# Even units: the second exponential ahead of x's rounding, and the second layer's Wq rounded in front of both

## Chip, core and metric

The kernel runs on one core of a Trainium2 chip. The metric is the time of one launch on the device in microseconds, as the median of several runs. An engine here is one of the core's five instruction streams: TensorE (PE in the rows; PEld are its weight loads), VectorE (DVE), ScalarE (ACT), GpSimd (POOL) and SyncE (SP), which issues the transfers.

## What is computed

Two layers of cross-attention, one behind the other, on x of 32 x 256 tokens by 320 channels, with a context of 32 x 77 rows by 512 channels. Each has 20 heads of 16 channels. The context has only the 77 text rows, so the parts of the reference for further rows are empty. Cut to what matters, in fp32:

```python
def layer(x, ctx, Wq, Wk, Wv, Wo, bo):
    q = heads(x @ Wq)                       # 20 heads of 16
    k, v = heads(ctx @ Wk), heads(ctx @ Wv)
    p = softmax(q @ k.T / sqrt(16))
    return merge(p @ v) @ Wo + bo + x

x = layer(x, ctx_2048, *L0)                 # weights of the first layer
x = layer(x, ctx_2048, *L1)                 # of the second
```

## The kernel before

Work goes in 32 **units** of 512 tokens (two batch elements), u = 0 to 31; units 0 to 15 are layer one, 16 to 31 layer two. Every product of matrices is done in two or three passes over a rounded value and the remainder that the rounding left. So each operand is **rounded** on ScalarE (`weight_hi`, line 611; `split_x`, line 629) and its **remainder** worked out on GpSimd (`weight_lo`, line 1224; `split_x`, line 1212). The rounding of x writes XS (line 636), and the two subtractions of GpSimd (lines 1217 and 1220) write the rest of XS. X32 has five buffers, which SyncE loads ahead; XS has one, so the rounding of unit u + 2 waits until the projections Q(u + 1, 0 to 2) are done with it.

Within a unit, the scores are made in five **runs**, run(u, k), k = 0 to 4. A run puts the scores of four heads for both batch elements, keys by tokens, into the four banks pA, with the row maxima taken off (lines 379 and 385), and beside them the scores of the next unit by tokens (line 366), of which VectorE takes those maxima (line 993). ScalarE's S(u, k) is the exponential of one run's four banks (line 742). The next run overwrites pA, so TensorE waits with run(u, k + 1) for S(u, k); and PV(u, k) (line 432) multiplies its result with V. The products go to SBUF, SyncE moves them into the natural order, the reciprocals of the sums are spread over DRAM (`<-rd`), GpSimd multiplies with them (`normalise`, line 1252), ScalarE rounds the result and out(u, m) (line 306 with Wo) projects it two units later.

The order on each engine is written out by hand, in one loop over u for each, with one branch for even and one for odd units. Engines meet over semaphores only; each engine works strictly in its own order. The stretch that the change touches, in an even unit u from 2 to 28:

- TensorE: run(u, 0), K(w, 0), K(w, 1), Q(u+1, 1), out(z, 1), run(u, 1), out(z, 0), V(w, 2), run(u, 2), out(z, 2), Q(u+2, 2), K(w, 2), with z = u - 2 and w = u/2 + 1; V and K are the context's projections. In unit 28 V(w, 2) is left out. Q(u+2, 2) waits for x's remainder (`x_lo`, line 318) and, in unit 14, for Wq's (`w_lo["Wq"]`).
- ScalarE: K(w, 1) and Q(u+1, 1) copies (KH, QH), then split_x(u+2), then S(u, 1), then v_half_copy (Vt, line 711), in unit 14 weight_hi("Wq", 1), then S(u, 2).
- GpSimd: split_o, split_x(u+2), in unit 14 weight_lo("Wq", 1), then normalise(u-1).
- VectorE: among others V(w, 2), which adds Vt (line 977), the maxima, and for K(w, 2) the products K_hi (line 907) and K_lo (line 917) out of Kt.

split_x on ScalarE begins with two waits, of which the first is for the load of x:

```python
act.wait_ge(d_x[x], 32 * (u // XR + 1))
if u:
    act.wait_ge(q_pe, all_of("Q", u - 1))
act.activation(XS[:, 0:3, :], X32[:, x, :, :], ACT.Copy).then_inc(x_hi, 1)
```

In odd units split_x(u+2) stands ahead of S(u, 1) too, and stays there.

Of the kernel before, what the change touches and what calls it, by code (L numbers as in the profile page):

```python
# [17 lines left out]
NCH = TOK // N  # L18
# [28 lines left out]
def build(nc, a):  # L47
    with ExitStack() as ctx:
        def sb(name, shape, dt=F32):
            return ctx.enter_context(nc.sbuf_tensor(name, shape, dt))  # L50
# [4 lines left out]
        Wq = sb("Wq", [128, 3, 2 * C], F32R)  # L55
# [554 lines left out]
        def _(act):  # L610
            def weight_hi(name, l):

                act.wait_ge(d_w[name], 16 * (l + 1))
                if l:

                    act.wait_ge({"Wk": k_pe, "Wv": v_pe, "Wq": q_pe, "Wo": o_pe}[name],
                                max(all_of(name[1].upper(), i) for i in range(NW // 2 if name in ("Wk", "Wv") else NCH)))
                src = staged(name, l)
                if name == "Wk":
                    act.activation(Wk[:, :, 0:C], src, ACT.Copy).then_inc(w_hi, 1)  # L620
                    return
                if name == "Wv":
                    act.activation(Wv[:, 0], src, ACT.Copy).then_inc(w_hi, 1)
                    return
                W = Wq if name == "Wq" else Wo
                act.activation(W[:, :, 256:C], src[:, :, 0:64], ACT.Copy)
                act.activation(W[:, :, 0:256], src[:, :, 64:C], ACT.Copy).then_inc(w_hi, 1)

            def split_x(u):
                if u >= NU:  # L630
                    return
                x = u % XR
# [4 lines that stand above are left out]
# [33 lines left out]
            def Q(u, m):  # L670

                if u >= NU:
                    return
                if m < 2:
                    act.wait_ge(q_pe, at["Q", u, m])
                    src, cols = psum(slot["Q", u, m])[:, :], slice(m * N, m * N + N)
                else:
                    act.wait_ge(q_summed, u + 1)
                    src, cols = Qt[:, 0:SQ], slice(2 * N, QC)
                if u > 1:  # L680
                    act.wait_ge(s_pe, NG * (u - 2) + (2, 4, 5)[m])
                act.activation(QH[:, u % 2, cols], src, ACT.Copy).then_inc(q_hi[m][u % 2], 1)
# [49 lines left out]
            def S(u, k):  # L732
                i = NG * u + k
                act.wait_ge(s_pe, i + 1)
                if i == 0:

                    for name in ("Wk", "Wq", "Wv"):
                        act.wait_ge(w_lo[name], 1)
                if i >= PR:

                    act.wait_ge(pv_pe, at["PV", (i - PR) // NG, (i - PR) % NG])
                act.activation(P[0:L, i % PR, :, :], pA[0:L, :, :], ACT.Exp, scale=float(D) ** -0.5).then_inc(p_done, 1)  # L742
# [42 lines left out]
            for u in range(NU - 1):  # L785
                n, v, z, w = u + 1, u - 1, u - 2, u // 2 + 1
                if u % 2 == 0:
                    split_o(z, 0)
                    S(u, 0)
                    split_o(z, 1)  # L790
                    if u == 0:
                        Q(1, 1)
                        v_half_copy(w)
                        split_x(2)
                        S(0, 1)
                        K(w, 1)
                    elif u < NU - 2:
                        K(w, 1)
                        Q(u + 1, 1)
                        split_x(u + 2)  # L800
                        S(u, 1)
                        if u < NU - 4:
                            v_half_copy(w)
                        if u == NCH - 2:
                            weight_hi("Wq", 1)
                    else:
                        Q(u + 1, 1)
                        S(u, 1)
                        v_half_copy(w - 1)
                        S(u, 2)  # L810
                        V_last(2)
                        q_half_copy(u + 1)
                        o_copy(u, 0)
                        S(u, 3)
                        split_o(v, 0)
                        o_copy(u, 1)
                        S(u, 4)
                        split_o(v, 1)
                        max_rows(n)
                        break  # L820
                    S(u, 2)
                    q_half_copy(u + 2)
                    k_half_copy(w)
                    o_copy(u, 0)
                    S(u, 3)
                    Q(u + 2, 0)
                    o_copy(u, 1)
                    if u == NCH - 4:
                        weight_hi("Wk", 1)
                    S(u, 4)  # L830
                    split_o(v, 0)
                    split_o(v, 1)
                    V(w, 1)
                    max_rows(n)
                else:
                    S(u, 0)
                    split_x(u + 2)
                    if u == NU - 3:
                        V_last(1)
                    S(u, 1)  # L840
                    S(u, 2)
                    o_copy(u, 0)
                    S(u, 3)
                    if u < NU - 3:
                        q_half_copy(u + 2)
                    o_copy(u, 2)
                    if u == NCH - 3:
                        weight_hi("Wv", 1)
                    S(u, 4)
                    Q(u + 2, 0)  # L850
                    if u == NCH + 1:
                        weight_hi("Wo", 1)
                    o_copy(u, 4)
                    max_rows(n)
# [344 lines left out]
        def _(pool):  # L1199
# [12 lines left out]
            def split_x(u):  # L1212
                if u >= NU:
                    return
                x = u % XR
                pool.wait_ge(x_hi, u + 1)
                pool.tensor_tensor(XS[:, 3:5, :], X32[:, x, 0:2, :], XS[:, 0:2, :].bitcast(F32), ALU.subtract).then_inc(x_lo, 1)  # L1217

                pool.wait_ge(x_lo, 2 * u + 1)
                pool.tensor_tensor(XS[64:128, 2, :], X32[64:128, x, 2, :], XS[64:128, 2, :].bitcast(F32),  # L1220
                                   ALU.subtract).then_inc(x_lo, 1)
                pool.wait_ge(x_lo, 2 * u + 2)
# [18 lines left out]
            def normalise(u, part):  # L1241
                if u < 0:
                    return
                if part == 0:
                    for r in range(2):
                        pool.wait_ge(d_on[r], 64 * (u + 1))
                    pool.wait_ge(d_rb, 32 * (u + 1))
                else:
                    pool.wait_ge(d_ont, 64 * (u + 1))
                    pool.wait_ge(d_rbt, 16 * (u + 1))  # L1250
                rows, blocks = (slice(0, 128), slice(0, 2)) if part == 0 else (slice(0, 64), slice(2, 3))
                pool.tensor_tensor(On[rows, blocks, :], On[rows, blocks, :], recips(u, part).bitcast(F32),  # L1252
                                   ALU.mult).then_inc(o_mul, 1)
# [21 lines left out]
            for u in range(NU):  # L1275
                if u % 2 == 0:
                    split_o(u - 2)
                    split_x(u + 2)
                    if u == NCH - 2:
                        weight_lo("Wq", 1)  # L1280
                    normalise(u - 1, 0)
                    normalise(u - 1, 1)
                    split_o(u - 1)
                    if u == NCH - 4:
                        weight_lo("Wk", 1)
                else:
                    split_c(u // 2 + 2)
                    split_x(u + 2)
                    if u == NCH - 3:
                        weight_lo("Wv", 1)  # L1290
                    normalise(u - 1, 0)
                    normalise(u - 1, 1)
                    if u == NCH + 1:
                        weight_lo("Wo", 1)
                    if u == NCH + 3:

                        pool.wait_ge(w_lo["Wo"], 2)
                        pool.memset(stage[:, :, :], 0.0).then_inc(nulls, 1)
# [273 lines left out]
```

## Time and profile before

| | us |
|---|---|
| median of 3 runs | 944.73 |
| lowest and highest of them | 940.63, 945.84 |
| the profiled execution | 941.04 |
| its span, first to last instruction | 939.2 |
| TensorE busy | 903.8 |
| VectorE busy | 686.2 |
| ScalarE busy | 544.1 |
| GpSimd busy | 400.0 |

Spans and waits below are of the profiled execution. 1.8 us of its time lie outside the span. An engine is counted busy while an instruction runs; TensorE's matmuls overlap each other, and the end of each is modelled, so that a wait of up to some 0.2 us behind a block may not be seen as idle.

### The profile page before, as it was taken

The numbers are of one execution on the slowest core, as the hardware profiler recorded it, in microseconds if no ns is written. First come the engines' busy times: TensorE is split into PE (matmuls) and PEld (weight loads), VectorE is DVE, ScalarE is ACT, GpSimd is POOL, SyncE is SP. The second block draws the span as 40 slices with busy tenths as digits, with TensorE's granted clock in tenths as the row PEclk, the third lists the DMA queues.
The fourth block names the chain that finished last, engine by engine and source line by source line (L and its number), as shares of the span: only waits on it lengthen the run. The fifth ranks groups of instructions, "written<-read, shape, count | busy, mean of one in ns | idle before, by whom it ended". The sixth has DMA issues, their size and how long they took to land.

```text
span 939.2 us, 28086 instructions
## 1 busy us (share of the span) xinstructions
PE 903.8 (96%) x11518; PEld 685.7 (73%) x11518; DVE 686.2 (73%) x1223; ACT 544.1 (58%) x547; POOL 400.0 (43%) x227
## 2 busy tenths in 40 slices
PE   8899999999999999998999999999999999999797
PEld 5777778777777877776677687777778777777564
DVE  4776786867678686686768778786787878677456
ACT  4456565656666565565466656566565656656452
POOL 3433354624435453365443456354344625422223
PEclk9999999999999999999999999999999999999999
DMA  6313434544453544544455444444544544444342
GB/s 212 89 34 93 132 99 113 142 127 132 104 142 90 160 133 120 139 117 121 122 145 140 106 108 128 132 131 123 132 107 110 132 128 133 113 116 98 94 107 84
DMA packets 80526, 112.41 MB, mean 120 GB/s; under 512 B 21200, under 2 KB 37878, under 8 KB 80400
## 3 DMA queue, kind: packets, MB, share of 16 engines
q1 hardware_dynamic: 80400, 110.61, 44.3%
q8 instruction: 94, 1.54, 0.7%
q14 instruction: 32, 0.26, 0.1%
HBM read 60.24 MB, written 22.24 MB: 88 GB/s over the span
## 4 chain that ended last, share of the span: by engine, by line
PE 49%; DMA 17%; SPq 15%; DVE 8%; issue 6%; ACT 3%; POOL 1%; DVEq 0%; ACTq 0%; POOLq 0%
PE pR L306 18%; PE pR L432 8%; PE pA L379 6%; SPq L1389 6%; PE pR L366 5%; DMA X<-y 5%; DMA X<-in_xT 4%; DMA y<-X 4%; PE pR L286 2%; SPq L1359 2%; SPq L1396 2%; DMA out<-X 2%; PE pR L256 2%; SPq L1423 2%; ACT P L742 2%
## 5 line engine op out<-in xcount | busy, mean ns | idle before, releaser
L742 ACT ACTIVATE P<-pA 77x2048 f32<-77x2048 f32 x160 | 300.3, 1877 | 166.8 <-PE pA L385 166.6
L993 DVE TENSOR_REDUCE Mx<-pR 128x4 f32<-128x308 f32 (+1 forms) x480 | 258.9, 575 | 32.7 <-PE pR L366 27.5
L1252 POOL TENSOR_TENSOR On<-On,OS 128x1024 f32<-128x1024 f32 (+1 forms) x58 | 105.7, 1844 | 276.7 <-DMA OS<-rd 276.6
L306 PE MATMUL pR<-OS,Wo 128*128 128x512 f32 x638 | 170.1, 406 | 4.1 <-DVE OS L1049 3.3
L306 PE MATMUL pR<-XS,Wq 128*128 128x512 f32 x638 | 168.5, 403 | 2.7 <-POOL Wq L1238 1.6
L432 PE MATMUL pR<-P,VA 77*17 77x256 f32 x2480 | 156.8, 383 | 2.2 <-DVE Mx L993 1.6
L366 PEld LDWEIGHTS pR<-KH,QH 32*128 32x128 f32 x1280 | 96.5, 183 | 78.2 <-issue 43.7
L366 PE MATMUL pR<-KH,QH 32*128 32x154 f32 x1280 | 132.0, 284 | 15.4 <-ACT P L742 7.4
L379 PE MATMUL pA<-QH,KH 32*77 32x256 f32 x1280 | 145.6, 292 | 0.1
L306 PEld LDWEIGHTS pR<-OS,Wo 128*128 128x128 f32 x638 | 114.7, 189 | 34.6 <-issue 4.8
L306 PEld LDWEIGHTS pR<-XS,Wq 128*128 128x128 f32 x638 | 116.3, 189 | 31.8 <-POOL Wq L1238 2.0
L379 PE MATMUL pA<-QL,KH 32*77 32x256 f32 x1280 | 135.5, 275 | 0.0
L379 PE MATMUL pA<-QH,KL 32*77 32x256 f32 x1280 | 135.3, 275 | 0.0
L1217 POOL TENSOR_TENSOR XS<-X,XS 128x1024 fp32r<-128x1024 f32 x31 | 74.1, 2389 | 143.0 <-ACT XS L636 143.0
L432 PEld LDWEIGHTS pR<-P,VA 77*17 77x17 f32 x2480 | 72.7, 112 | 66.9 <-issue 33.2
L385 PE MATMUL pA<-Mt,neg 32*77 32x256 f32 x1280 | 101.2, 277 | 0.0
L1060 DVE SCALAR_TENSOR_TENSOR X<-pR,bias,X 128x512 f32<-128x512 f32 (+1 forms) x93 | 69.0, 743 | 43.4 <-PE pR L306 42.7
L379 PEld LDWEIGHTS pA<-QL,KH 32*77 32x77 f32 x1280 | 91.6, 142 | 0.0
L379 PEld LDWEIGHTS pA<-QH,KL 32*77 32x77 f32 x1280 | 91.0, 141 | 0.0
L1259 POOL TENSOR_TENSOR OS<-On,OS 128x1024 fp32r<-128x1024 f32 x31 | 74.1, 2390 | 29.9 <-ACT OS L765 29.9
L379 PEld LDWEIGHTS pA<-QH,KH 32*77 32x77 f32 x1280 | 84.1, 141 | 2.2 <-issue 1.6
L385 PEld LDWEIGHTS pA<-Mt,neg 32*77 32x77 f32 x1280 | 77.4, 140 | 0.0
(154 smaller groups left out, 1215.2 us busy)
## 6 DMA issues: line engine op xcount, KB each, us to landing
On<-Oraw SPq DMA_DIRECT2D x248, 64.0 KB, 2.7
OS<-rd SPq DMA_DIRECT2D x58, 256.0 KB
C<-in_cT SPq DMA_DIRECT2D x16, 616.0 KB, 8.0
X<-in_xT SPq DMA_DIRECT2D x16, 512.0 KB
y<-X SPq DMA_DIRECT2D x16, 512.0 KB, 4.2
X<-y SPq DMA_DIRECT2D x16, 512.0 KB
out<-X SPq DMA_DIRECT2D x15, 512.0 KB, 4.2
X<-in_xT SPq DMA_DIRECT2D x16, 256.0 KB
```

The lines of the kernel that those rows point to most:

```text
L306: f = pe.matmul(p[:, :], W[:, k, c0:c0 + 128], S[:, s, :], start=(i == 0), stop=(i == len(pairs) - 1))
L366: return pe.matmul(pR[:, (second if j > 1 else first) + j % 2, t * LK:t * LK + LK], QH[32 * j:32 * j + 32, n % 2, c0:c0 + 128], kt, start= ...
L379: pe.matmul(pA[0:L, j, h * SQ:h * SQ + SQ], kt[:, pp * L:pp * L + L], Q_[32 * j:32 * j + 32, u % 2, c0:c0 + SQ], start=(i == 0), stop=Fals ...
L385: return pe.matmul(pA[0:L, j, h * SQ:h * SQ + SQ], neg[32 * j:32 * j + 32, i:i + 1].broadcast_to([32, L]), Mt[32 * j:32 * j + 32, :], star ...
L432: f = pe.matmul(bank[32 * j:32 * j + D + 1, b * SQ:b * SQ + SQ], VA[0:L, u % 2, b, h:C + H:H], src, start=True, stop=True, skip_group_chec ...
L742: act.activation(P[0:L, i % PR, :, :], pA[0:L, :, :], ACT.Exp, scale=float(D) ** -0.5).then_inc(p_done, 1)
L993: dve.tensor_reduce(Mx[:, :, :].rearrange("p t (j i) -> p j t i", j=4)[:, j:j + banks, :, i:i + 2], pR[:, bank:bank + banks, 0:2 * LK].rea ...
L1060: dve.scalar_tensor_tensor(out=X32[0:M, x, m, :], in0=p[0:M, :], scalar=bias[0:M, l, m:m + 1], in1=X32[0:M, x, m, :], op0=ALU.add, op1=ALU ...
L1217: pool.tensor_tensor(XS[:, 3:5, :], X32[:, x, 0:2, :], XS[:, 0:2, :].bitcast(F32), ALU.subtract).then_inc(x_lo, 1)
L1252: pool.tensor_tensor(On[rows, blocks, :], On[rows, blocks, :], recips(u, part).bitcast(F32), ALU.mult).then_inc(o_mul, 1)
L1259: pool.tensor_tensor(OS[:, 3:5, :], On[:, 0:2, :], OS[:, 0:2, :].bitcast(F32), ALU.subtract).then_inc(o_lo, 1)
L1389: sp.dma_start(On[32 * j + D * r:32 * j + D * r + D, 0:2, :], Oraw[32 * j:32 * j + D, r:r + 3:2, :]).then_inc(d_on[r], 16)
```

## The change

Two things, both in even units. On ScalarE, S(u, 1) now comes ahead of split_x(u + 2) in units 2 to 28. In unit 14, weight_hi("Wq", 1) comes ahead of both, and on GpSimd weight_lo("Wq", 1) comes ahead of split_x(16). The instructions, their number and their operands are the same.

```diff
                     elif u < NU - 2:
                         K(w, 1)
                         Q(u + 1, 1)
+                        if u == NCH - 2:
+                            weight_hi("Wq", 1)
+                        S(u, 1)
                         split_x(u + 2)
-                        S(u, 1)
                         if u < NU - 4:
                             v_half_copy(w)
-                        if u == NCH - 2:
-                            weight_hi("Wq", 1)
                     else:
...
                 if u % 2 == 0:
                     split_o(u - 2)
-                    split_x(u + 2)
                     if u == NCH - 2:
                         weight_lo("Wq", 1)
+                    split_x(u + 2)
                     normalise(u - 1, 0)
```

On ScalarE, in unit 2, as it was (P is the output of an exponential, XS of x's rounding, Vt of v_half_copy):

```order
L653 ACTIVATE KH<-pR,mask 128x4x77 x2
L682 ACTIVATE QH<-pR 128x512
L636 ACTIVATE XS<-X 128x1536
L742 ACTIVATE P<-pA 77x2048
L711 ACTIVATE Vt<-pR 52x320
L742 ACTIVATE P<-pA 77x2048
```

And as it is now:

```order
L653 ACTIVATE KH<-pR,mask 128x4x77 x2
L682 ACTIVATE QH<-pR 128x512
L742 ACTIVATE P<-pA 77x2048
L636 ACTIVATE XS<-X 128x1536
L711 ACTIVATE Vt<-pR 52x320
L742 ACTIVATE P<-pA 77x2048
```

The rounding has moved behind the exponential, and stands between it and the copy of Vt; the other even units are alike.

On ScalarE in unit 14, as it was:

```order
L682 ACTIVATE QH<-pR 128x512
L636 ACTIVATE XS<-X 128x1536
L742 ACTIVATE P<-pA 77x2048
L711 ACTIVATE Vt<-pR 52x320
L626 ACTIVATE Wq<-stage 128x3x64
L627 ACTIVATE Wq<-stage 128x3x256
L742 ACTIVATE P<-pA 77x2048
```

And now:

```order
L682 ACTIVATE QH<-pR 128x512
L626 ACTIVATE Wq<-stage 128x3x64
L627 ACTIVATE Wq<-stage 128x3x256
L742 ACTIVATE P<-pA 77x2048
L636 ACTIVATE XS<-X 128x1536
L711 ACTIVATE Vt<-pR 52x320
L742 ACTIVATE P<-pA 77x2048
```

Both activations of Wq have moved ahead of the exponential and the rounding of x.

On GpSimd in unit 14, the only difference on that engine:

```order
 L1252 TENSOR_TENSOR On<-On,OS 64x512
 L1259 TENSOR_TENSOR OS<-On,OS 128x1024
-L1217 TENSOR_TENSOR XS<-X,XS 128x1024
-L1220 TENSOR_TENSOR XS<-X,XS 64x512
 L1237 TENSOR_TENSOR Wq<-stage,Wq 128x3x64
 L1238 TENSOR_TENSOR Wq<-stage,Wq 128x3x256
+L1217 TENSOR_TENSOR XS<-X,XS 128x1024
+L1220 TENSOR_TENSOR XS<-X,XS 64x512
```

Wq's two subtractions now precede x's. TensorE, VectorE and SyncE keep their order.

## Rows read from the trace of the kernel before

**Rows 1.** The page: busy time of the engine, and its granted clock by fortieths.

```profile
PE 903.8 (96%) x11518; PEld 685.7 (73%) x11518; DVE 686.2 (73%) x1223; ACT 544.1 (58%) x547; POOL 400.0 (43%) x227
...
PEclk9999999999999999999999999999999999999999
```

**Rows 2.** Who waited for whom, TensorE: total us, times, longest us.

```profile
PE pR L366 <- ACT P L742: 7.4, 7, 1.7
```

**Rows 3.** Timeline, unit 2: start us, us, engine, line, out<-in, [idle before <-releaser].

```profile
100.34 1.49 ACT L636 ACTIVATE XS<-X 128x1536 fp32r<-128x1536 f32 x1 [1.29 <-DMA X<-in_xT]
...
101.56 2.08 PE L306 MATMUL pR<-OS,Wo 128*128 128x512 f32 x8
...
101.91 2.40 POOL L1217 TENSOR_TENSOR XS<-X,XS 128x1024 fp32r<-128x1024 f32 x1 [6.59 <-ACT XS L636]
...
104.39 1.29 POOL L1220 TENSOR_TENSOR XS<-X,XS 64x512 fp32r<-64x512 f32 x1
...
104.83 0.43 ACT L711 ACTIVATE Vt<-pR 52x320 f32<-52x320 f32 x1 [1.23 <-PE pR L278]
...
107.64 1.30 PE L306 MATMUL pR<-XS,Wq 128*128 128x512 f32 x5
...
114.40 3.64 POOL L1252 TENSOR_TENSOR On<-On,OS 128x1024 f32<-128x1024 f32 x2 [8.72 <-DMA OS<-rd]
```

**Rows 4.** Timeline, unit 6, where x's load is late.

```profile
212.51 1.49 ACT L636 ACTIVATE XS<-X 128x1536 fp32r<-128x1536 f32 x1 [3.85 <-DMA X<-in_xT]
...
215.81 0.34 PE L366 MATMUL pR<-KH,QH 32*128 32x154 f32 x2 [1.40 <-ACT P L742]
```

**Rows 5.** Timeline, ScalarE in odd unit 13: an exponential, the rounding, the next exponential.

```profile
404.80 1.88 ACT L742 ACTIVATE P<-pA 77x2048 f32<-77x2048 f32 x1 [4.00 <-PE pA L385]
406.58 1.47 ACT L636 ACTIVATE XS<-X 128x1536 fp32r<-128x1536 f32 x1
408.34 1.88 ACT L742 ACTIVATE P<-pA 77x2048 f32<-77x2048 f32 x1 [0.29 <-PE pA L385]
```

**Rows 6.** Timeline, unit 14.

```profile
423.65 0.37 SPq L1311 DMA_DIRECT2D stage<-in_Wq  x1
...
443.77 1.80 POOL L1238 TENSOR_TENSOR Wq<-stage,Wq 128x768 fp32r<-128x768 f32 x1
...
445.63 2.29 PE L306 MATMUL pR<-XS,Wq 128*128 128x512 f32 x5 [1.55 <-POOL Wq L1238]
...
451.48 3.62 POOL L1252 TENSOR_TENSOR On<-On,OS 128x1024 f32<-128x1024 f32 x2 [5.90 <-DMA OS<-rd]
451.56 3.64 DVE L907 TENSOR_SCALAR KH<-Kt,mask 128x154 fp32r<-128x154 f32 x2
...
455.73 1.08 PE L432 MATMUL pR<-P,VA 77*17 77x256 f32 x16 [1.62 <-DVE Mx L993]
```

**Rows 7.** Timeline, unit 28, which has no V block.

```profile
829.05 2.08 PE L306 MATMUL pR<-OS,Wo 128*128 128x512 f32 x8
...
832.06 0.34 PE L366 MATMUL pR<-KH,QH 32*128 32x154 f32 x2 [0.94 <-ACT P L742]
...
834.67 1.31 PE L306 MATMUL pR<-XS,Wq 128*128 128x512 f32 x5
```

**Rows 8.** DMA issues: out<-in, how many, KB each, median us to landing.

```profile
stage<-in_Wq SPq DMA_DIRECT2D x1, 480.0 KB, 5.2
```

**Rows 9.** Timeline, unit 10, around the products of line 917.

```profile
329.17 1.32 PE L306 MATMUL pR<-XS,Wq 128*128 128x512 f32 x5
329.41 1.92 SPq L1423 DMA_DIRECT2D OS<-rd  x3
...
334.24 0.66 DVE L917 SCALAR_TENSOR_TENSOR KL<-Kt,mask,KH 128x154 fp32r<-128x154 f32 x2
...
335.06 2.39 POOL L1252 TENSOR_TENSOR On<-On,OS 128x1024 f32<-128x1024 f32 x1 [6.67 <-DMA OS<-rd]
```

**Rows 10.** Windows: stretch, its us, TensorE busy, granted clock, DMA share, GB/s.

```profile
445.90:449.30 3.40, 3.40 (x12) 0.50 0.81 238
```

## The prediction

> **What bounds the kernel now.** I read the page first. TensorE is busy for 903.8 of 939.2 us and its clock is at the upper of its two levels (2.4 GHz) nearly everywhere [rows 1]. So TensorE is the bound, and the question is only what the 35 us are in which it isn't busy. Next the list of who waited for whom, for TensorE alone [rows 2]. The largest entry belongs to the order that is changed: before the score matmuls (line 366) it waits for the exponential (line 742) seven times, 7.4 us in all. Its two entries of 1.6 us, for GpSimd's Wq and for a maximum on VectorE, both stand in unit 14 [rows 6].
>
> Then the timeline of an even unit, since only those change. I count from **r**, the start of the eight-matmul block of out(z, 0), right behind run(u, 1). In unit 2 r is 101.56 [rows 3]. ScalarE rounds x at 100.34. GpSimd works out x's remainder from 101.91 to 105.68, and TensorE starts Q(u+2, 2) at 107.64, r + 6.08, without waiting. So in such a unit TensorE has 2.0 us in hand at Q over x's remainder. In unit 6 the load of x is late: ScalarE sits 3.85 us until it lands at 212.51, with the exponential queued behind the rounding, and TensorE loses 1.40 us before run(u, 2) [rows 4]. This is the real fault of the old order. The other six waits of that entry are of the same kind, in units 10, 12, 14, 22, 26 and 28.
>
> **Part 1: the exponential ahead of the rounding, in the fourteen even units 2 to 28.** What is removed: all seven waits. S(u, 1) starts when the run ends, as in odd units, which is r, and takes 1.88 us; TensorE wants the scores' bank behind its V block, which in unit 2 ends at about r + 3.2, when Vt is copied [rows 3, 5]. That is **-7.4 us** [rows 2].
>
> What is added: the rounding can't start before the exponential has let go. In odd units the next activation starts 1.78 us behind an exponential's start [rows 5]. The chain to Q is then, from r, where the exponential starts: 1.78 to the rounding, 1.57 from the rounding's start to GpSimd's (100.34 to 101.91), 3.77 for its two subtractions (101.91 to 105.68), and 0.06 from GpSimd's end to the first matmul (445.57 to 445.63) [rows 3, 5, 6]. Sum: **r + 7.2**. TensorE would be there at r + 6.08. So it waits 1.1 us at Q(u+2, 2), in every even unit, late load or not: the late loads of the trace all land before r + 1.8 (unit 6: r + 1.35), so they no longer count [rows 4]. Thirteen times 1.1 is 14.3 us. Unit 28 has no V block, and reaches Q 4.68 us behind r once its 0.94 us wait is taken off (829.05 to 834.67) [rows 7]; there the new wait is 2.5 us. **+16.8 us** together. Nothing downstream takes this up, as TensorE runs from Q to the next r without a wait that is worth naming in ordinary units.
>
> Also moved behind the rounding is v_half_copy, and VectorE's addition of V stands behind it, for which run(u, 2) waits at its ninth step. It would start at r + 3.2; in unit 2 it starts at r + 3.27, being held by TensorE's own V block [rows 3]. Cost nothing; if V's block were shorter it would be late by the difference. SyncE's queue is not touched.
>
> The Trainium skill (Perfetto Trace Analysis, Optimization Strategies) advises to work on those engines for which TensorE sits idle. By that alone the blocking exponential goes first and the change is worth the 7.4 us of its entry. The trace differs, in that an engine for which TensorE doesn't wait now, with 2.0 us in hand, is put 3.1 us back.
>
> **Part 2: Wq of the second layer, once, in unit 14.** Before, its rounding stands behind v_half_copy and its remainder on GpSimd behind x's; Q waits 1.55 us for it [rows 6]. Now ScalarE does it behind its copy of Q, in the idle stretch in which it waited for x, from about 434. By then TensorE's last use of the old Wq is over, since that is what that copy waits for, and the new one has landed (issued at 423.65, 5.2 us to landing) [rows 6, 8]. Two activations take 1.2 us and GpSimd's two subtractions 2.4 us, so Wq is done by about 437.9, before x's turn at 440. **-1.6 us**, and nothing is added: both engines are idle in that stretch.
>
> **What hangs on these waits.** Unit 14 has another 1.62 us wait of TensorE at 455.73, for a maximum. Its cause stands in the rows: at 451.48 GpSimd began its two multiplications of On, and VectorE's two small products at 451.56 took 3.64 us together, where the next pair, which does more, takes 0.66 in unit 10 [rows 6, 9]. They met there because Q was late and slow while the multiplications were not. With Wq in time they shouldn't meet: **-1.6 us**. And the granted clock: it is 0.50 from 445.9 to 449.3, right behind the waits of unit 14 [rows 6, 10]. One other fall like it stands at 384, behind the 1.7 us wait of unit 12 [rows 2]; the 1.40 us of unit 6 were not followed by any [rows 4]. 3.4 us at 1.2 instead of 2.4 GHz cost 1.7 us each. With waits of 1.1 us I take both as gone: **-3.4 us**.
>
> **The sum.** 16.8 - 7.4 - 1.6 - 1.6 - 3.4 = **+2.8 us**. Two terms have no row and lie between bounds. First, the meeting of GpSimd's multiplications with VectorE's products: VectorE's second pair (line 917) follows Q by 5.07 to 5.73 us (unit 10: 334.24 against 329.17), so it moves to r + 12.3 to 12.9. The multiplications don't follow Q, but the broadcast that SyncE issues when out(z, 2) is done. In unit 10 they came 5.65 us behind the issue, which would put them at r + 12.0, on top of the pair; in unit 2 at r + 12.84, just behind the start of its second half [rows 3, 9]. Each meeting costs between nothing and the 1.6 us of unit 14. I take three units (10, 22, 26, where that delay is short) at half the price, some +1 us (bounds 0 and 14 x 1.6 = 22). Second, the 2.5 us wait of unit 28 may bring the clock down for 3.4 us, as 1.7 us did: 0 to 1.7, I take +0.8. Total **+4 us** or so, +0.4%.
>
> **Against which time.** The profiled execution took 941.0 us; with +4 it comes to 945. The median of the three runs is 3.7 us above it. If those 3.7 us are later loads and falls of the clock, the change takes them away as well, and 945 stays; if not, they are added, and it is 948.7. I take the middle, **947 us**.
>
> **The rivals.**
> Pile-up, slower: the multiplications meet VectorE's products in half of the even units, 7 x 1.6 = 11 us on top of 2.8, so **955**. For it: a margin of some 0.3 us in units like 2. Against: the pair's second half has begun by then. It decides if GpSimd starts before about r + 12.6.
> The Trainium skill (GPSIMD Engine Reference, Specifications) names this contention: GpSimd's SBUF interfaces are shared with VectorE, and the two contend where VectorE's instruction is in a two-port mode or has two SBUF inputs. By that every instruction of line 917 that overlaps is held, and a unit in which they overlap pays unit 14's price, not nothing.
> Milder: late loads make up most of the scatter of the runs, and no meeting occurs: 941.0 + 2.8, **944**, within 0.5% too. For it: all of the old waits come from landing times. Against: nothing shows what the slower runs held.
> Free rounding, faster: the delayed remainder isn't awaited, since TensorE is behind elsewhere in ordinary units. Then only the gains stand, 941.0 - 7.4 - 1.6 = **932**. Against it stands the sum r + 7.2, all of whose terms repeat within 0.1 us; only a TensorE that reaches Q 1 us later than in unit 2 would do.
> The old trouble kept: the loads land later than r + 1.8 in many units. Then rounding and Q wait for them as before, and only the P waits go; this is part of the range's lower half.
>
> **How the numbers follow.** Forecast 0.60, pile-up 0.17, milder 0.16, free rounding 0.07. About 0.5%, or 4.7 us, is what a measurement tells from no change. Faster by more needs under 940: free rounding and a hair of the milder case, 0.08. Slower by more needs over 949.4: the pile-up and a quarter of the forecast, 0.32. Within, 0.60. The range reaches from 942 (milder, at the low end of the runs) to 954, leaving out free rounding and the worse half of the pile-up.
>
> **What would show it.** TensorE's wait for the exponential at line 366 falls from 7.4 us to about nothing. A new entry stands in its place: line 306 waiting for GpSimd's L1220, fourteen times, 0.9 us each (the idle time shown is some 0.2 less than the delay, as the block before is drawn longer), over 12 us in all. ScalarE no longer waits for loads of x in even units. Wq's entry vanishes, and the clock has no fall near 384 and 446, perhaps one behind unit 28. The products of line 917 longer than 0.4 us each would be the pile-up. If the new entry is under 5 us, the chain to Q was wrong, and the time is under 940.

## The result, and the profile after

| | us |
|---|---|
| before, median of 7 runs | 945.46 (940.63 to 948.51) |
| after, median of 7 runs | 951.67 (948.62 to 955.03) |
| after over before | 1.0076, 95% interval 1.0047 to 1.0106 |
| the profiled execution, before and after | 941.04, 952.77 |

The change makes the kernel slower by 0.76%. The forecast was 947, between 942 and 954, with a chance of 0.60 on a change of under 0.5% and 0.32 on a loss of over 0.5%. So the time lies in the range, but it was the less likely of the two outcomes that came. The two profiled executions are 11.7 us apart, where the medians are 6.2 us apart; where these 11.7 us lie is worked out below.

TensorE's waits after the change, the rows that answer to [rows 2] (who waited for what: total us, times, longest us):

```profile
PE pR L306 <- POOL XS L1220: 9.8, 13, 1.3
PE pR L366 <- DVE Mx L993: 6.1, 4, 2.0
PE pR L366 <- DVE X L1060: 5.7, 7, 1.2
```

The exponential is gone from before line 366. Three other entries stand where it was. The first is GpSimd's remainder of x, at Q. The second and third were small before (0.3 and 1.0 us). From here on **Q** is the first matmul of Q(u+2, 2), and r is as in the prediction.

The timeline of unit 2 after the change, which answers to [rows 3]:

```profile
101.89 2.08 PE L306 MATMUL pR<-OS,Wo 128*128 128x512 f32 x8
101.93 1.88 ACT L742 ACTIVATE P<-pA 77x2048 f32<-77x2048 f32 x1 [2.54 <-PE pA L385]
103.71 1.47 ACT L636 ACTIVATE XS<-X 128x1536 fp32r<-128x1536 f32 x1
...
105.26 2.38 POOL L1217 TENSOR_TENSOR XS<-X,XS 128x1024 fp32r<-128x1024 f32 x1 [9.91 <-ACT XS L636]
...
107.71 1.27 POOL L1220 TENSOR_TENSOR XS<-X,XS 64x512 fp32r<-64x512 f32 x1
...
109.03 1.19 PE L306 MATMUL pR<-XS,Wq 128*128 128x512 f32 x4 [0.85 <-POOL XS L1220]
```

r is 101.89 here. The exponential starts at r + 0.04, the rounding at r + 1.82, GpSimd ends at r + 7.09, and Q starts at r + 7.14, where it stood at r + 6.08 before. The visible wait is 0.85 us.

Unit 4 shows the second entry:

```profile
169.74 3.70 POOL L1252 TENSOR_TENSOR On<-On,OS 128x1024 f32<-128x1024 f32 x2 [4.99 <-DMA OS<-rd]
169.98 3.64 DVE L917 SCALAR_TENSOR_TENSOR KL<-Kt,mask,KH 128x154 fp32r<-128x154 f32 x2
173.54 0.79 DVE L993 TENSOR_REDUCE Mx<-pR 128x8 f32<-128x616 f32 x1
174.58 0.34 PE L366 MATMUL pR<-KH,QH 32*128 32x154 f32 x2 [1.86 <-DVE Mx L993]
```

GpSimd's multiplications begin 0.24 us ahead of VectorE's pair of line 917. The pair takes 3.64 us instead of 0.66 [rows 9], the maximum behind it comes late, and TensorE waits 1.86 us. I call this a meeting. Taken singly, the first product ran to 0.18 us behind the end of GpSimd's first multiplication (2.34 us instead of 0.37), and the second to 0.18 us behind the end of the second one (1.38 us). Units 26 and 28 have a meeting each, too, with waits of 2.0 us. Unit 26 from behind Q to 794.8, with that wait in it, and what followed, in windows (us, TensorE busy, granted clock, DMA share, GB/s):

```profile
786.00:794.80 8.80, 6.77 (x121) 1.00 0.68 195
794.90:798.20 3.30, 3.30 (x9) 0.50 0.42 146
```

The wait of 2.03 us ended at 793.34, and from 794.9 the granted clock was at the lower of its two levels (1.2 GHz) for 3.4 us. The same stands at 852.9, behind the meeting of unit 28.

### The profile page after: what moved, and what is told of

Same layout as the page of the kernel before. It is cut to its first block, busy times and chain, and to the rows that moved or that the text cites. A ratio compares the mean times of both kernels' runs of the same rounds, so it can differ in the third digit from the quotient of the medians.

```text
span 951.0 us, 28086 instructions
## 1 busy us (share of the span) xinstructions
PE 906.4 (95%) x11518; PEld 684.9 (72%) x11518; DVE 685.9 (72%) x1223; ACT 543.8 (57%) x547; POOL 399.7 (42%) x227
## 4 chain that ended last, share of the span: by engine, by line
PE 64%; DMA 8%; DVE 7%; SPq 7%; POOL 6%; issue 5%; ACT 4%; DVEq 0%; POOLq 0%; ACTq 0%
PE pR L306 22%; PE pR L432 13%; PE pA L379 8%; PE pR L366 6%; PE pR L286 4%; DMA X<-in_xT 3%; POOL XS L1217 3%; PE pR L256 3%; ACT XS L636 2%; SPq L1389 2%; DMA y<-X 2%; PE pA L385 2%; POOL XS L1220 2%; PE pR L260 1%; DVE KL L917 1%
## 5 line engine op out<-in xcount | busy, mean ns | idle before, releaser
L306 PE MATMUL pR<-XS,Wq 128*128 128x512 f32 x638 | 170.6, 407 | 11.4 <-POOL XS L1220 9.8
```

The lines of the kernel that those rows point to most:

```text
L306: f = pe.matmul(p[:, :], W[:, k, c0:c0 + 128], S[:, s, :], start=(i == 0), stop=(i == len(pairs) - 1))
```

## The experiments

Each was timed in turn with the kernel before, on the same chip. Ratios are to that kernel, in brackets the 95% interval; the change has 1.0076 (1.0047 to 1.0106). The runs were made on three chips (e1 to e4, e5 to e8, e9 to e11), so that ratios compare better than medians do.

| run | what | us, median | ratio |
|---|---|---|---|
| e1 | exponential first alone | 955.56 | 1.0126 (1.0096 to 1.0156) |
| e2 | Wq alone | 941.58 | 0.9968 (0.9938 to 0.9998) |
| e3 | rounding one step later | 999.35 | 1.0599 (1.0570 to 1.0628) |
| e4 | change, K(w, 2) before Q | 933.38 | 0.9899 (0.9873 to 0.9925) |
| e5 | before, K(w, 2) before Q | 942.11 | 0.9980 (0.9951 to 1.0009) |
| e6 | change, products early | 954.97 | 1.0129 (1.0086 to 1.0171) |
| e7 | change, unit 28 as before | 952.01 | 1.0080 (1.0050 to 1.0109) |
| e8 | e2 with K(w, 2) before Q | 942.60 | 0.9972 (0.9945 to 0.9999) |
| e9 | change, multiplications after products | 945.63 | 1.0029 (1.0003 to 1.0056) |
| e10 | change, out(z, 0) before the reciprocals | 952.55 | 1.0103 (1.0067 to 1.0139) |
| e11 | e4 with e10's swap | 931.44 | 0.9884 (0.9855 to 0.9913) |

### The two parts apart: e1 and e2

e1 is the change with Wq's rounding and remainder at their old places:

```diff
-                        if u == NCH - 2:
-                            weight_hi("Wq", 1)
                         S(u, 1)
                         split_x(u + 2)
                         if u < NU - 4:
                             v_half_copy(w)
+                        if u == NCH - 2:
+                            weight_hi("Wq", 1)
```

and on GpSimd split_x(u + 2) ahead of weight_lo("Wq", 1) again. e2 is the converse: the kernel before, with Wq's two steps moved ahead of x's on both engines.

> The exponential ahead of x's rounding alone; Wq of the second layer as before. Chain theory (GpSimd's remainder of x is done at r + 7.1 in every even unit, and Q(u+2, 2) waits for it): as the change, and in unit 14 Q also waits for Wq's remainder, which starts only at r + 7.1 and takes 2.4 us, so Q at r + 9.5 and some 2.4 us more than the change, 4 with a fall of the clock: 954 to 956 where the change has 951.7 and before 945.5. Rival (the loss of the change comes from GpSimd's multiplications meeting VectorE's products, and not from Q): TensorE's waits for L1220 cost nothing, and the time differs from the change only by meetings, 948 to 955.

> Wq's rounding and remainder ahead of x's in unit 14 alone; x's rounding still ahead of the exponential in all units. Theory: the 1.55 us wait for Wq, the 1.6 us wait for a maximum (whose cause was the meeting of GpSimd's multiplications with VectorE's products in unit 14) and perhaps a fall of the clock go: 4 us under before, 941 to 942. Rival: the wait for the maximum has another cause and stays: 1.5 to 2 us under before.

e1 took 955.56 us. Its waits of TensorE:

```profile
PE pR L306 <- POOL XS L1220: 11.1, 13, 1.4
PE pR L366 <- DVE Mx L993: 7.9, 6, 2.1
...
PE pR L306 <- POOL Wq L1238: 3.3, 1, 3.3
```

As expected, in unit 14 Q waits for Wq's remainder, 3.3 us; this alone makes e1 slower than the change. It also has six meetings where the change's profile had three, which the theory left open. The time is within the theory's 954 to 956, and so near the rival's 955 that it doesn't part the two.

e2 took 941.58 us, within what was expected. In unit 14 of its profile:

```profile
435.50 1.84 POOL L1238 TENSOR_TENSOR Wq<-stage,Wq 128x768 fp32r<-128x768 f32 x1
...
438.72 1.49 ACT L636 ACTIVATE XS<-X 128x1536 fp32r<-128x1536 f32 x1 [3.85 <-DMA X<-y]
...
442.02 0.49 PE L366 MATMUL pR<-KH,QH 32*128 32x154 f32 x2 [2.40 <-ACT P L742]
```

Wq is done at 437.3, long ahead of its use, while x's late load and the exponential behind it still cost 2.40 us. Behind that wait the granted clock was at 1.2 GHz for 6.8 us (a window with its us, TensorE busy, granted clock, DMA share, GB/s):

```profile
441.80:448.40 6.60, 6.38 (x50) 0.50 0.08 18
```

Of the meeting of unit 14 [rows 6] nothing is left. So the second part is a gain of about 0.3%, at an interval that nearly reaches 1, and the first one is a loss of some 1%, by the change over e2 (1.0076 against 0.9968). e1's 1.3% holds the wait for Wq as well.

### Is it Q that waits? e3 and e4

e3 puts the rounding yet one step back. It adds more of the suspected delay.

```diff
                         S(u, 1)
-                        split_x(u + 2)
                         if u < NU - 4:
                             v_half_copy(w)
+                        split_x(u + 2)
```

> The change, with x's rounding put one step further back, behind the copy of Vt, in units 2 to 26. Chain theory: the copy waits for the V block until r + 3.3, so the rounding starts at r + 3.6 instead of r + 1.8, and Q(u+2, 2) at r + 8.9 instead of 7.15, 1.8 us more in thirteen units: 23 us over the change, 975; with a fall of the clock behind each wait of 2.8 us up to 1.7 us more per unit, 997. Rival (Q's wait is covered by something else): within 5 us of the change.

e4 leaves the chain as it is and gives TensorE work in front of Q. The order is changed in the same way on three engines, and the two banks change places, so that each is read early enough for run(u, 3):

```diff
 # TensorE
-                    Q(u + 2, 2, 3)
-                    K(w, 2, 0)
+                    K(w, 2, 3)
+                    Q(u + 2, 2, 0)
 # ScalarE
-                    q_half_copy(u + 2)
                     k_half_copy(w)
+                    q_half_copy(u + 2)
 # VectorE
-                    q_sum(u + 2)
                     k_sum(w)
+                    q_sum(u + 2)
```

> The change, with K(w, 2) ahead of Q(u+2, 2) on TensorE, ScalarE and VectorE, and their two banks swapped: 1.3 us of matmuls that need no x stand between out(z, 2) and Q. Chain theory: TensorE comes to Q at r + 7.4, GpSimd is done at 7.1, so the waits for L1220 (9.8 us in the profile of the change) go, some 14 us of delay; the waits for VectorE before run(u, 2), 5.7 us, which lay under Q's wait, now count: 10 us under the change, 941 to 942, and less if fewer products of VectorE meet GpSimd's multiplications: 936. Rival (meetings and clock cause the loss): no more than 2 us from the change unless the products of line 917 stop being held.

e3 took 999.35 us, 2.4 us above the upper end of what was expected. Its largest wait, unit 2 of its timeline, and the clock in units 2 and 4:

```profile
PE pR L306 <- POOL XS L1220: 32.1, 13, 2.7
```

```profile
110.40 1.95 PE L306 MATMUL pR<-XS,Wq 128*128 128x512 f32 x5 [2.68 <-POOL XS L1220]
```

```profile
111.10:114.40 3.30, 3.30 (x16) 0.50 0.89 256
169.20:175.80 6.60, 6.07 (x29) 0.50 0.86 258
```

Q starts 8.9 us behind r (101.49), as worked out, and in eleven of the thirteen units a stretch at 1.2 GHz begins during or right behind the wait. It lasts 3.4 us in seven of them and 6.8 us in the four of units 4, 12, 14 and 16, which the expectation hadn't allowed for. The profile has one more, at 261, so twelve between 100 and 840 us. Between r and Q e3's profile has 22.5 us more than the change's. What the clock takes can be estimated from each run's mean granted clock and its span, as (1 - clock) times the span: 27.7 us in the mean of e3's five runs and 5.7 in that of the change's seven, so 22 us more.

e4 took 933.38 us, 1.0% or 11 us under the kernel before on the same chip, and by the ratios 1.8% or 17 us under the change. This was better than the 936 to 942 expected. Unit 2 of e4:

```profile
106.48 1.39 PE L306 MATMUL pR<-OS,Wo 128*128 128x512 f32 x5
107.42 1.29 POOL L1220 TENSOR_TENSOR XS<-X,XS 64x512 fp32r<-64x512 f32 x1
107.71 0.73 PE L243 MATMUL pR<-CS,Wk 128*128 128x308 f32 x4
...
108.28 0.72 PE L246 MATMUL pR<-CS,Wk 128*64 128x308 f32 x4
...
108.84 1.36 PE L306 MATMUL pR<-XS,Wq 128*128 128x512 f32 x5
```

GpSimd still ends at r + 7.1 (101.59 is r), but TensorE does K(w, 2) meanwhile and starts Q at r + 7.25 without a wait. And the pair of line 917 now ends earlier against the multiplications:

```profile
112.82 0.65 DVE L917 SCALAR_TENSOR_TENSOR KL<-Kt,mask,KH 128x154 fp32r<-128x154 f32 x2
114.45 2.40 POOL L1252 TENSOR_TENSOR On<-On,OS 128x1024 f32<-128x1024 f32 x1 [5.74 <-DMA OS<-rd]
```

The pair ends at r + 11.9 and no even unit from 2 on has a meeting, so e4 takes off both losses at once. By the same estimate the clock takes 3.0 us in e4's runs and 5.6 in those of the kernel before beside them, so 2.6 of the 11 us are the clock's. e3 and e4 speak for the wait at Q; how much of e4's gain is the meetings needs e9.

### Is it the swap alone? e5 and e8

e5 is the kernel before with e4's swap; e8 is e2 with it. Neither moves the exponential.

> The kernel before, with K(w, 2) ahead of Q(u+2, 2) and their banks swapped, as in e4, and nothing else: x's rounding is still ahead of the exponential, Wq behind both. Theory (the exponential's delay costs some 7 us by itself, and only the cover at Q lets the change keep them): Q wasn't awaited in the old order but once, so the swap gives it little, 0 to 3 us under before, most of it Wq's wait in unit 14: 942 to 944. Rival (the swap is what makes e4 fast, whatever the order of the exponential, for instance since VectorE's products move away from GpSimd's multiplications): as e4, 933 to 936.

> e4 with x's rounding back ahead of the exponential: Wq early and K(w, 2) ahead of Q(u+2, 2), the old order else. Theory: TensorE's waits for the exponential behind late loads come back, 7 to 8 us over e4, 940 to 942, and this difference is what the exponential ahead of the rounding is worth once Q's wait is covered. Rival (the exponential's place is worth nothing and e4's gain is the swap): 933 to 935, as e4.

They took 942.11 us, at the lower edge of the theory's 942 to 944, and 942.60 us, 0.6 above its 940 to 942; both are far from e4's 933. TensorE's wait for the exponential is back in both, 9.6 us in e5 and 7.0 in e8:

```profile
PE pR L366 <- ACT P L742: 9.6, 10, 2.0
```

```profile
PE pR L366 <- ACT P L742: 7.0, 8, 1.6
```

So the swap alone is worth nothing that these runs can tell from no change (0.9980, 0.9951 to 1.0009), and the exponential's place alone costs 1%. Both together gain 1%. e4 over e8, 0.9899 against 0.9972, is what the first part of the change is worth once its cost is covered: 0.7%, or 7 us, the size of the term of 7.4 [rows 2].

### The meetings: e6 and e9

e6 moves VectorE's products ahead of the maxima, out of reach of the multiplications:

```diff
                     k_sum(w)
-                    maxima(n, 3, 0)
                     K_hi(w, 2)
-                    maxima(n, 3, 1)
                     K_lo(w, 2)
-                    maxima(n, 3, 2)
+                    maxima(n, 3, 0, 1, 2)
```

> The change, with VectorE's products of lines 907 and 917 put together right behind the sum of Kt, ahead of the three maxima of the fourth run, so that line 917 ends at r + 11.9 instead of 13.0, before GpSimd's multiplications can begin (earliest r + 12.1 in the profile of the change). Theory: the meetings (three in that profile, 1.9 us each, two with a fall of the clock behind) go, Q's waits for L1220 stay: 944 to 948, 4 to 8 us under the change. Rival (only Q's wait matters and the meetings are absorbed): 950 to 952.

It took 954.97 us, a miss for both theories. Its profile has no meeting from unit 2 on, but a new entry:

```profile
PE pR L306 <- DVE Mx L993: 10.0, 19, 0.6
```

That entry was 1.2 us in the change's profile. The next Q(u+2, 0) takes a bank whose maximum now comes 0.6 us later, in each of fourteen units. These waits took up what the missing meetings gave back, and more by the medians, so e6 doesn't price the meetings. e9 does, by letting GpSimd wait and leaving VectorE alone:

```diff
                     split_x(u + 2)
+                    if u and u < NU - 2:
+                        pool.wait_ge(k_lo[2], u // 2 + 2)
                     normalise(u - 1, 0)
```

> The change, with one wait more on GpSimd: in even units its multiplications start only when VectorE has finished the products of line 917 (r + 13.0). So no meeting can occur, and unlike e6 VectorE's order is untouched; the multiplications move by at most 0.9 us. Theory: the meetings cost about 2 us each and sometimes a fall of the clock; the change had three in its profile, e1 six, e7 five: 4 to 8 us under the change, 944 to 948. Rival (meetings cost nothing on the whole, as e6 seems to say, whose time rose): 951 to 953.

It took 945.63 us, in the range of the theory, with a ratio of 1.0029 (1.0003 to 1.0056) against the change's 1.0076 (1.0047 to 1.0106). That is 4.4 us less; from the two intervals I estimate some 4 us of uncertainty on it either way, so that the sign is shown and the size is not. TensorE's waits for line 306 stay, and those for line 993 before line 366 are gone from the head of the list:

```profile
PE pR L306 <- POOL XS L1220: 11.0, 13, 0.9
PE pR L306 <- DVE OS L1049: 2.6, 2, 1.7
```

And GpSimd's own list says how often the new wait was the last to end:

```profile
POOL On L1252 <- DVE KL L917: 60.3, 10, 6.0
```

(The 60.3 us are all of its idle time ahead of these ten, most of it spent waiting for data anyway.) In ten of fourteen units the data had landed before r + 13.1, so a meeting is a near thing in most units, and when the DMA lands decides: there are three in the change's profile, six in e1's, five in e7's and five in e10's. In all of these 19 the first multiplication began before the second product of line 917 did, by 0.04 us at the least; where it began 0.04 us or more behind that, the pair took its usual 0.66 us. Where only one of the two products was caught (in nine of the 19 the second, in two the first) the pair took 2.5 to 2.8 us and TensorE waited 0.7 to 1.1 us, not 2. The waits of a profile's meetings add up to 5.9, 7.9, 5.7 and 6.3 us.

### Two smaller questions: e7, and e10 with e11

e7 leaves unit 28 in the old order, for which the prediction had the largest wait.

> The change, with unit 28 alone in the old order, x's rounding ahead of the exponential. Theory: in unit 28 the change moves Q from r + 5.6 to r + 7.15; 1.5 us, and up to 1.7 us of a fall of the clock and 2 us of a meeting, if these stand in unit 28: 1.5 to 5 us under the change, 947 to 950. Rival (the last units have slack, since TensorE waits 2 to 3 us for a remainder of line 1049 in unit 30 anyway): as the change, 951 to 952.

It took 952.01 us, ratio 1.0080 (1.0050 to 1.0109), the same as the change and at the upper end of its rival's 951 to 952. Its unit 28 loses 1.8 us to the exponential in its own profile, and it had five meetings. A gain of 1.5 us is below what this resolves; one of 5 us is excluded. Whether slack in the last units takes up the rest stays open.

e10 and e11 put out(z, 0) ahead of the two reciprocals on VectorE, on the change and on e4:

```diff
                         maxima(n, 1, 1, 0, 2)
+                        out(z, 0)
                         recip_last(v)
                         recip(v)
-                        out(z, 0)
```

> The change, with VectorE's out(z, 0) ahead of its two reciprocals, whose inputs come late by DMA. Theory: TensorE's waits for line 1060 before run(u, 2), 5.7 us in seven units of the change's profile, go, but they lie under the wait at Q, which GpSimd ends at r + 7.15 whatever TensorE does before: within 1 us of the change, 951 to 953, unit 28 giving nothing either. Rival (waits add up): 5 to 6 us under the change, 946.

> e4 with the same swap on VectorE. With Q's wait covered, TensorE's waits for line 1060 are its own: 2.5 us in e4's profile, so 2 to 3 us under e4's 933.4, 930 to 932. Rival (the later reciprocals hold up the broadcast and so the multiplications, and come back as waits for line 1049 or 252): 933 or more.

e10 took 952.55 us. The entry for line 1060 before line 366 has fallen from 5.7 us to 0.9 (unit 28's alone), and that for L1220 has grown from 9.8 to 11.5 us:

```profile
PE pR L306 <- POOL XS L1220: 11.5, 13, 1.2
```

A wait was exchanged for another, and the time is that of the change, as expected. e11 took 931.44 us, within the 930 to 932 expected. It is 1.9 us by the medians under e4, though the intervals overlap. It is the fastest of all, 1.2% under the kernel before.

## Why the prediction was right, and where not

**The chain to Q: right.** It was worked out at r + 7.2, and twelve of the fourteen units have Q within 7.14 to 7.21. Units 10 and 14 have 7.36 and 7.59: there the load of x let the rounding start only at r + 2.0 and r + 2.2, later than the r + 1.8 by which the prediction had all loads landed. Thirteen waits were shown (9.8 us) where fourteen were forecast with over 12; unit 14's is down as "issue". They are smaller than forecast in units 8, 10, 12 and 14, where TensorE was held earlier, by line 1060. The sum of all delays between r and Q rose by 7.3 us over the fourteen units. The prediction's terms give 16.8 - 7.4 - 1.6, less 0.9 for the part of the clock's fall in unit 12 that lay before Q: 6.9.

**The 7.4 us: right as an entry, incomplete as a reading.** The wait for the exponential is gone. The prediction said that TensorE would then run on to Q. In seven places it waits for line 1060 instead, 5.7 us. Unit 14, after:

```profile
443.40 0.55 DVE L1014 RECIPROCAL Zg<-Zg 128x64 f32<-128x64 f32 x1 [1.69 <-DMA Zg<-Oraw]
443.87 0.65 DVE L1060 SCALAR_TENSOR_TENSOR X<-pR,bias,X 128x512 f32<-128x512 f32 x1
...
444.67 0.34 PE L366 MATMUL pR<-KH,QH 32*128 32x154 f32 x2 [1.25 <-DVE X L1060]
```

VectorE sits in front of a reciprocal whose input is late, with out(z, 0) queued behind it. In unit 28 this wait lay under the exponential's: line 1060 ended at r + 2.9 in both profiles, so the 0.94 us there were never to be had. In units 8, 10, 12 and 14 it is mostly new: the reciprocal started between r + 1.6 and 2.4 before and between r + 2.8 and 3.2 after. e1's profile has three such waits, 2.2 us in all, so they differ between profiles; whether the change makes them more frequent stays open. They cost nothing here, since GpSimd holds Q until r + 7.1 anyway: e10 shows it.

**Wq: right.** In unit 14 it is done at 441.1, before r + 1. Q's wait for it and the meeting at 451 are gone. e2 shows the gain, about 0.3%.

**The meetings: right in kind, the term mis-sized.** The prediction took three units at half of 1.6 us, +1 us. There were three in the profile (4, 26 and 28, not 10, 22 and 26), at 1.9 to 2.0 us, so 5.9 us. e9 puts the meetings, with what they do to the clock, at 4.4 us of the change's time, with the uncertainty named there. The step that failed is the use of the landing time of single units as if it were theirs: it changes from run to run, and most units are within reach. Two sizes in it were right. The pair moved to r + 12.3, and the bound of about r + 12.6 for GpSimd's start is the start of its second product. The pile-up rival had the mechanism, with seven meetings and 11 us; three to six and 4 to 8 us were found. Its stronger form, in which every product of line 917 that overlaps a multiplication is held, is not borne out: in unit 6 the second product had begun 0.22 us ahead of the multiplication, overlapped it and kept its length.

**The clock: the gain didn't come.** -3.4 us were booked for two falls that wouldn't come. At 384 and 446 they didn't, but two of the meetings were followed by falls of their own, at 794.9 and 852.9, for the same 3.4 us, and the profile has one more at 934.8, behind a wait of 1.3 us near the end, that the profile of before hadn't. By the estimate from the mean granted clocks, the clock takes 5.7 us in the change's runs and 5.6, 6.1 and 4.8 in those of the kernel before on the three chips of the experiments: no gain. Waits of 0.85 us at Q were not followed by a fall; the longer ones of e3 were, in eleven units. The +0.8 us for a fall behind unit 28's wait at Q is not borne out either: that wait was drawn at 1.3 us, and the fall at 852.9 came 10 us later, behind the meeting.

**The sum.** It gave +4 us for the profiled execution, and the medians moved by 6.2. With the meetings at 4.4 instead of 1 it would have been some 7. e9, the change without meetings, is 0.29% or 2.8 us slower than the kernel before, and the sum without its last two terms was +2.8 us; that they agree this well is luck, given e9's interval and a clock term that the runs don't show. The two single profiles are 11.7 us apart: 7.3 between r and Q, 7.4 in the three stretches with a meeting, two of them with a fall (from Q to the r of the next even unit they take 50.6 to 52.1 us, where their like before took 48.7 to 49.1), 4.1 less in the stretches of units 12 and 14, and 1.4 us at the start and the end. The profile of after lies near the top of its runs and that of before near the bottom. Taking the middle between the profiled time and the median was a guess, and it is partly by luck that 951.67 lies inside the range. The milder case, in which the change takes the scatter away, is not borne out, as the runs of after spread over 6.4 us and those of before over 7.9.

## What to carry to other kernels

A wait that is taken away in front of the busiest engine is worth something only if no other chain moves back by more than it has in hand; before two steps in an engine's queue are swapped, count both chains to the point at which the busy engine needs them. When the swap costs a fixed delay, look for work of the busy engine that doesn't depend on the delayed data: 1.1 us of it turned a loss of 0.8% into a gain of 1.0%. And where a short instruction of one engine and a long one of another are closer to each other than the landing times scatter, one profile doesn't tell how often they meet.

## What the runs showed of the hardware

- Two VectorE instructions of 0.66 us together, which read only SBUF, took 3.6 to 3.8 us in the change when GpSimd's multiplications had begun just ahead of them. Each ended some 0.2 us behind the multiplication that ran beside it. Where only the second was caught they took 2.8 us (e1, e7, e10). A product that had begun 0.04 us or more before the multiplication kept its length, and in unit 16, where it had begun 0.1 us before, the multiplication took 2.53 us instead of 2.39. The product of line 946, 0.29 us alone, took up to 1.3 us where a multiplication was running (unit 22). The maxima of line 993, which read PSUM, and the addition of line 977, which reads PSUM and SBUF, kept their length (line 977 took 0.48 us at 105.77, beside GpSimd's subtraction from 105.26 to 107.64). This was in the kernel before too [rows 6], and no run of this case shows which of the operands decides.
- TensorE's granted clock fell to 1.2 GHz for 3.4 us behind waits of 1.97 and 2.03 us in the change and of 1.7 us in unit 12 before, and in e3 at eleven of the thirteen waits of 1.7 to 2.7 us in units 2 to 26, there for 3.4 or 6.8 us. It fell for 3.4 us behind e1's 3.3 us and for 6.8 us behind e2's 2.4 us, both in unit 14. It didn't fall behind the 1.86 us of unit 4, nor behind two of the 2.7 us in e3 (units 8 and 20), nor behind any wait of 0.85 us at Q. It fell behind none of the meetings of e1, e7 and e10, whose waits reached 2.1 us. So the length of one wait alone doesn't decide it. I estimate the cost of a fall of 3.4 us at 1.7 us beside the wait, from the two levels, where TensorE is busy throughout.
